# First cross-attention loop: the key projection moved two batches ahead, between the transposes and the products with the values

## The reference, cut to what matters

```python
Q = (query @ w_q.T).reshape(b, sq, NUM_HEADS, D_K).transpose(0, 2, 1, 3)
K = (key @ w_k.T).reshape(b, sk, NUM_HEADS, D_K).transpose(0, 2, 1, 3)
V = (value @ w_v.T).reshape(b, sk, NUM_HEADS, D_K).transpose(0, 2, 1, 3)
scores = jnp.einsum('bhqd,bhkd->bhqk', Q, K) / scale
scores = scores + _alibi_bias(sq, sk, scores.dtype)[None]
attn = jax.nn.softmax(scores, axis=-1)
ctx = jnp.einsum('bhqk,bhkd->bqhd', attn, V).reshape(b, sq, D_MODEL)
return ctx @ w_o.T + b_o
```

## Time and profile before

| | us |
|---|---|
| Median of three runs | 1930.89 |
| Their lowest and highest | 1924.9, 1931.84 |
| The profiled execution | 1929.83 |
| Span of its trace | 1928.2 |
| PE busy over the span | 1672.4 (87%) |
| DVE, ACT, POOL busy | 1059.2, 755.5, 746.0 |

### The profile page before, as it was taken

How to read it: one execution, slowest core, us unless ns; L and a number is a source line. 1 busy time by engine, 2 the same in 40 slices (tenths; PEclk the granted TensorE clock), 3 DMA queues, 4 the chain that set the end, 5 groups by cost and what they waited for, 6 DMA issues and landing times.

```text
span 1928.2 us, 24024 instructions
## 1 busy us (share of the span) xinstructions
PE 1672.4 (87%) x8816; PEld 806.3 (42%) x8816; DVE 1059.2 (55%) x1548; ACT 755.5 (39%) x1191; POOL 746.0 (39%) x452
## 2 busy tenths in 40 slices
PE   7888886886999999999997769999803979899998
PEld 4666663541222232222224525444401557644443
DVE  2444444465998998998993333222368464422121
ACT  1333332275776776776771222111414240122121
POOL 0433331238998998998993010000000023000000
PEclk8999997788999999999999668999855879699999
DMA  2111101003000100100102400111071100100110
GB/s 68 33 33 33 33 27 53 0 14 104 8 19 7 28 16 8 30 13 8 31 5 67 176 0 1 49 33 33 15 168 39 33 0 1 45 9 35 44 44 22
DMA packets 37895, 66.64 MB, mean 35 GB/s; under 512 B 13764, under 2 KB 24408, under 8 KB 36260
## 3 DMA queue, kind: packets, MB, share of 16 engines
q1 hardware_dynamic: 34612, 64.47, 11.3%
q10 hardware_dynamic: 3200, 1.07, 0.2%
HBM read 56.33 MB, written 9.20 MB: 34 GB/s over the span
## 4 chain that ended last, share of the span: by engine, by line
PE 51%; POOL 22%; DVE 12%; issue 11%; DMA 2%; ACT 2%; SPq 1%; DVEq 0%; ACTq 0%; POOLq 0%
POOL arena L1247 20%; PE ps L1467 6%; PE ps L2203 6%; PE ps L2214 6%; PE ps L201 3%; PE ps L1480 3%; PE ps L342 3%; PE ps L347 3%; PE ps L224 3%; PE ps L360 2%; DVE arena L477 2%; PE ps L1978 2%; PE ps L1994 2%; DVE arena L488 1%; PE ps L217 1%
## 5 line engine op out<-in xcount | busy, mean ns | idle before, releaser
L1247 POOL TENSOR_TENSOR arena<-arena 128x768 f32<-128x768 f32 x248 | 532.4, 2187 | 23.2 <-DVE arena L1164 23.2
L867 PE MATMUL ps<-arena 32*128 32x512 f32 x1520 | 316.7, 653 | 0.9 <-ACT arena L1052 0.9
L1167 DVE TENSOR_TENSOR arena<-arena,ps 128x1024 f32<-128x1024 f32 x248 | 302.1, 1218 | 10.2 <-POOL arena L1247 5.5
L2160 POOL TENSOR_TENSOR arena<-arena 128x1024 f32<-128x1024 f32 x16 | 30.0, 1896 | 433.3 <-DVE arena L2093 418.6
L1045 ACT ACTIVATE arena<-arena 128x1024 f32<-128x1024 f32 x124 | 131.1, 1057 | 136.3 <-DVE arena L1147 136.3
L1147 DVE TENSOR_TENSOR arena<-arena,ps 128x1024 f32<-128x1024 f32 x124 | 151.4, 1221 | 22.0 <-PE ps L878 9.5
L915 PE MATMUL ps<-arena 128*32 128x512 f32 (+15 forms) x1024 | 136.9, 607 | 10.4 <-DVE arena L1167 9.9
L1052 ACT ACTIVATE arena<-ps 128x1024 f32<-128x1024 f32 x124 | 127.0, 1024 | 24.8 <-PE ps L867 9.7
L1054 ACT ACTIVATE arena<-arena 128x1024 f32<-128x1024 f32 x124 | 131.1, 1057 | 3.9
L1467 PE MATMUL ps<-arena 128*128 128x512 f32 x288 | 131.9, 602 | 0.5 <-ACT arena L1532 0.5
L867 PEld LDWEIGHTS ps<-arena 32*128 32x128 f32 x1520 | 103.3, 186 | 65.3 <-issue 58.6
(11 more groups left out here) (306 smaller groups left out, 2400.6 us busy)
## 6 DMA issues: line engine op xcount, KB each, us to landing
arena<-ctxT SPq DMA_DIRECT2D x32, 257.0 KB, 3.0
arena<-ctxT SPq DMA_DIRECT2D x8, 1028.0 KB, 15.7
arena<-L_ffn_w SPq DMA_DIRECT2D x16, 512.0 KB, 4.3
arena<-ctx_rows SPq DMA_DIRECT2D x8, 960.0 KB
arena<-L_ffn_eW SPq DMA_DIRECT2D x8, 512.0 KB, 3.7
m_rows<-arena SPq DMA_DIRECT2D x12, 256.0 KB, 2.8
arena<-m_rows SPq DMA_DIRECT2D x32, 64.0 KB
m_yd<-arena SPq DMA_DIRECT2D x64, 32.0 KB, 2.3
```

The costliest lines, as they stand in the source:

```text
L867: mm = nc.tensor.matmul(ps[:, bank + jj, :], weights[r], m_row[r, n // CH % 2, n % CH, :], start=start, stop=True)
L1167: nc.vector.tensor_tensor(m_h[:, u, n % 2], m_xa[:, u, n % 2], ps[:, bank:bank + 2, :], ALU.add).then_inc(S["m_use"], 1)
L1247: nc.gpsimd.tensor_tensor(x, x, m_h[:, u, (n - 1) % 2].rearrange("p j d -> p (j d)")[:, own], ALU.mult).then_inc(S["m_kept"], 1)
```

## The change

- PE's list for a batch is now: scores of b + 1, transposes of b, keys of b + 2, value products of b, values of b + 2. Before the loop the keys and values of batches 0 and 1 are both projected.
- The keys of the 256 first context rows go to one bank (6) and the values to bank 4, which the transposes use too. So the transposes of b now also wait until the values of b + 1 have been copied out.
- The key of the last context row is projected ahead of the loop for all batches, with the last value row (eight more small matrix instructions in the trace). It is put into column 256 of `kT` by a new POOL copy of 128x2 elements for each batch, behind the query blocks, and the wait for the queries counts three events instead of two. POOL begins its first query block only when these projections have been copied out.
- DVE's list becomes: maxima of b + 1, copy of the transposed half of b, reciprocal of b + 1, output of b, copy of the values of b + 2. ACT's: copy of the transposed half, exponentials, copy of the keys.

```diff
+            for n, w in enumerate((x0["wv"], x0["wk"])):
+                for m in range(DC):
+                    o = (DC * n + m) * B
+                    for k in range(DC):
+                        mm = nc.tensor.matmul(ps[:, 0, o:o + B], w[:, k, m * P:(m + 1) * P],
+                                              x0["cl"][:, k, :], start=(k == 0), stop=(k == 1))
...
-            with pe.Fori(0, B // 2 - 1) as i:
-                b = 2 * i
-                proj(b + 1, 1, i)
-                scores(b + 1, 1)
-                tail(b, 0)
-                proj(b + 2, 0, i + 1)
-                scores(b + 2, 0)
-                tail(b + 1, 1)
-            proj(B - 1, 1, B // 2 - 1)
+            keys(1, 1, 0)
+            values(1, 1)
+            with pe.Fori(0, B // 2 - 1) as i:
+                for j in range(2):
+                    b = 2 * i + j
+                    scores(b + 1, 1 - j)
+                    turn(b, j)
+                    keys(b + 2, j, i + 1)
+                    weigh(b, j)
+                    values(b + 2, j)
...
+                nc.gpsimd.tensor_copy(x0["kT"][j][:, :, SK - 1:SK], x0["kl"][:, :, bass.ds(b, 1)]).then_inc(S["x_qblk"], 1)
```

More of the change, by code:

```diff
@@ L57 @@
 SHARED = ([(0, f"slot_ctx{j}", f"x_ctx{j}", 16 * (B // 2)) for j in range(2)]
-         + [(0, "tile_qblk", "x_qblk", DC * B), (0, "tile_norm", "x_norm", B), (0, "tile_rec", "x_rec", B)]
+         + [(0, "tile_qblk", "x_qblk", (DC + 1) * B), (0, "tile_norm", "x_norm", B), (0, "tile_rec", "x_rec", B)]
          + [(0, "once_1", "x_vl", 1), (0, "once_2", "x_vlast", 1)]
@@ L280, in build @@
             slope=bview(22 * K + 16, 4, P), pos=bview(22 * K + 16 + 256, SK + 1),
-            cl=view(37 * K, DC, B), vl=view(37 * K + 64, DC, B),
+            cl=view(37 * K, DC, B), vl=view(37 * K + 64, DC, B), kl=view(37 * K + 128, DC, B), vkl=view(37 * K + 64, 2 * DC * B),
             slope32=view(36 * K, 4, P), pos32=view(36 * K + 512, SK),
@@ L325, in x_pe, with keys, values @@
             pe.wait_ge(*S.at("xq_ev_d", 4))
[L327 to L330, removed]
-            mm.then_inc(S["x_vl"], 1)
-            def proj(b, j, i):
+            for n, w in enumerate((x0["wv"], x0["wk"])):
[4 more added lines that the diff above has]
+                                              x0["cl"][:, k, :], start=(k == 0), stop=(k == 1))
+            mm.then_inc(S["x_vl"], 1)
+            def keys(b, j, i):
+                pe.wait_ge(*S.at(f"x_ctx{j}", 16 * (i + 1)))
+                if not isinstance(b, int) or b >= 1:
+                    pe.wait_ge(*S.at("x_kev", b))
+                for m in range(DC):
+                    for k in range(DC):
+                        mm = nc.tensor.matmul(ps[:, 6, m * (SK - 1):(m + 1) * (SK - 1)], x0["wk"][:, k, m * P:(m + 1) * P],
+                                              x0["ctx"][j][:, k, 0:SK - 1], start=(k == 0), stop=(k == 1))
+                mm.then_inc(S["x_k"], 1)
+            def values(b, j):
                 if not isinstance(b, int) or b >= 1:
                     pe.wait_ge(*S.at("x_vev", b))
[L337 to L344, removed]
                 for t in range(2):
                     for k in range(DC):
-                        mm = nc.tensor.matmul(ps[:, 6, t * D:(t + 1) * D], cx[:, k, t * P:(t + 1) * P],
+                        mm = nc.tensor.matmul(ps[:, 4, t * D:(t + 1) * D], x0["ctx"][j][:, k, t * P:(t + 1) * P],
                                               x0["wv"][:, k, :], start=(k == 0), stop=(k == 1))
@@ L353, in scores @@
                 pe.wait_ge(*S.at("x_kev", b + 1))
-                pe.wait_ge(*S.at("x_qblk", 2 * b + 2))
+                pe.wait_ge(*S.at("x_qblk", 3 * b + 3))
                 if not isinstance(b, int) or b >= 1:
@@ L366, in scores, with turn @@
                 mm.then_inc(S["x_s"], 1)
-            def tail(b, j):
+            def turn(b, j):
                 pe.wait_ge(*S.at("x_norm", b + 1))
+                pe.wait_ge(*S.at("x_vev", min(b + 2, B) if isinstance(b, int) else b + 2))
                 for t in range(2):
@@ L376, in tail, with weigh @@
                     mm.then_inc(S["x_pt"], 1)
+            def weigh(b, j):
                 pe.wait_ge(*S.at("x_or", b + 1))
@@ L386, in tail @@
                 mm.then_inc(S["x_o"], 1)
-            proj(0, 0, 0)
+            keys(0, 0, 0)
+            values(0, 0)
             pe.wait_ge(*S.at("x_alibi", 4))
             scores(0, 0)
+            keys(1, 1, 0)
+            values(1, 1)
             with pe.Fori(0, B // 2 - 1) as i:
-                b = 2 * i
-                proj(b + 1, 1, i)
-                scores(b + 1, 1)
-                tail(b, 0)
-                proj(b + 2, 0, i + 1)
-                scores(b + 2, 0)
-                tail(b + 1, 1)
-            proj(B - 1, 1, B // 2 - 1)
+                for j in range(2):
[5 more added lines that the diff above has]
+                    values(b + 2, j)
             scores(B - 1, 1)
-            tail(B - 2, 0)
-            tail(B - 1, 1)
+            turn(B - 2, 0)
+            weigh(B - 2, 0)
+            turn(B - 1, 1)
+            weigh(B - 1, 1)
             pe.wait_ge(*S.at("x_or", B + 1))
@@ L423, in keys @@
                 act.wait_ge(*S.at("x_k", b + 1))
-                nc.scalar.copy(x0["kT"][j], ps[:, 4:6, 0:SK]).then_inc(S["x_kev"], 1)
+                nc.scalar.copy(x0["kT"][j][:, :, 0:SK - 1],
+                               ps[:, 6, :].rearrange("p (m s) -> p m s", m=DC)).then_inc(S["x_kev"], 1)
             def exps(b, j):
@@ L439, in x_act @@
             exps(0, 0)
+            keys(1, 1)
             with act.Fori(0, B // 2 - 1) as i:
[L441 to L448, removed]
+                for j in range(2):
+                    b = 2 * i + j
+                    turned(b)
+                    exps(b + 1, 1 - j)
+                    keys(b + 2, j)
             turned(B - 2)
@@ L465, in x_dve @@
             ch.link(nc.vector.tensor_reduce(x0["par"], hmask.rearrange("p (a i) -> p i a", i=2), AX.X, ALU.add))
-            nc.vector.tensor_copy(x0["vl"].rearrange("p c b -> p (c b)"), ps[:, 0, 0:DC * B]).then_inc(S["x_vlast"], 1)
+            nc.vector.tensor_copy(x0["vkl"], ps[:, 0, 0:2 * DC * B]).then_inc(S["x_vlast"], 1)
             for r in (slice(0, 6), slice(64, 70)):
@@ L472, in values @@
                 dve.wait_ge(*S.at("x_v", b + 1))
-                nc.vector.tensor_copy(x0["v"][j].rearrange("p a b -> p (a b)"), ps[:, 6, :]).then_inc(S["x_vev"], 1)
+                nc.vector.tensor_copy(x0["v"][j].rearrange("p a b -> p (a b)"), ps[:, 4, :]).then_inc(S["x_vev"], 1)
             def maxima(b, j):
@@ L484, in sums, with turned, outs @@
                 nc.vector.reciprocal(x0["st"][j][:, 2, :], x0["st"][j][:, 1, :]).then_inc(S["x_rec"], 1)
-            def outs(b):
+            def turned(b):
                 dve.wait_ge(*S.at("x_pt", 2 * b + 2))
                 nc.vector.tensor_copy(x0["pT"][:, 1, :], ps[:, 5, :]).then_inc(S["x_pt1ev"], 1)
+            def outs(b):
                 dve.wait_ge(*S.at("x_o", b + 1))
@@ L501, in x_dve @@
             sums(0, 0)
+            values(1, 1)
             with dve.Fori(0, B // 2 - 1) as i:
[L503 to L512, removed]
+                for j in range(2):
+                    b = 2 * i + j
+                    maxima(b + 1, 1 - j)
+                    turned(b)
+                    sums(b + 1, 1 - j)
+                    outs(b)
+                    values(b + 2, j)
             maxima(B - 1, 1)
+            turned(B - 2)
+            sums(B - 1, 1)
             outs(B - 2)
-            sums(B - 1, 1)
             dve.wait_ge(*S.at("x_norm", B))
@@ L520, in x_dve @@
                                         x0["own"].unsqueeze(1).broadcast_to([P, B, L]), ALU.mult).then_inc(S["x_spread"], 1)
+            turned(B - 1)
             outs(B - 1)
@@ L558, in normed @@
                                         ALU.mult).then_inc(S["x_norm"], 1)
+            pool.wait_ge(*S.at("x_vlast", 1))
             qblk(0, 0)
```

## The result

| | before | after |
|---|---|---|
| Median of the runs | 1931.19 us (4 runs) | 1896.52 us (4 runs) |
| Lowest to highest | 1924.9 to 1931.84 | 1893.49 to 1897.95 |
| Profiled execution, its span | 1929.83, 1928.2 | 1896.26, 1894.6 |
| Scores of batch 1 to scores of batch 31 | 244.10 | 208.75 |

The ratio after to before is 0.9826, with an interval of 0.9802 to 0.9849: the changed kernel is faster by 1.7%. The gain is 34.7 us by the medians where 29 had been forecast.

What follows compares the result with a forecast made beforehand. PE was taken to bound the loop; its terms summed to 7.16 us per batch against 8.137, so 1929.83 - 29.3 + 0.9 = 1901.4 us, stated as 1902 for the median, range 1896 to 1911.

Steps and rivals of the forecast that it cites:

- PE bounds the loop and loses time at L383 and at the branch: In the loop: PE is busy 14.55 of 16.28 us per two batches and loses time between its instructions.
- Both waits go: Before the value products: PE's waits for ACT's copy (0.40 us) and DVE's copy (0.30 us) should vanish.
- The branch goes under: At the loop's end: the branch's 0.38 us per pair of batches is hidden behind the values, taken as 0.
- Scores 1.70, transposes 0.96, keys 1.84, values 1.94: PE's forecast us per batch for these four pieces of the loop in the new order.
- rival B: In PE's loop: the new seams between pieces are dear, giving 7.40 us per batch and 1909 us; chance 0.12.
- Value products 0.72: In PE's loop: each half of the value products costs 0.36 us once unhindered, 0.72 us per batch.
- 1898 to 1910 of the bounds: Whole kernel: time in us by the bounds alone, with a batch between 7.04 and 7.40 us.
- Ahead of the loop + 0.9: Before the loop: eight more small instructions on PE's path add 0.9 us, upper bound 1.08.
- Nothing else is late: In the loop: softmax, copies and transfer finish before they are wanted, the softmax with 1.2 us to spare.
- POOL's copy 0: In the loop: the new 128x2 copy runs in POOL's idle 4.75 us per batch, 0 on the path.
- D: In the loop: PE's clock falls to 1.2 GHz, making the kernel slower, 1942 to 1959 us; chance 0.03.
- Later stages only shift: Behind the loop: later stages are taken as shifted only, without changing their lengths.

Runs made afterwards that it cites:

- experiment 1: Changed kernel with the keys of b + 2 put back behind the value products; 1925.9 us, ratio to before 0.9983.
- experiments 2 and 3: PE's loop written as 5 turns of 6 batches: in the kernel before, 1925.2 us; in the changed kernel, 1894.1 us.
- experiment 8: Changed kernel with keys and value products cut in halves and interleaved; 1906.3 us, ratio to before 0.9865.
- experiments 5 and 6: Changed kernel with DVE's output ahead of its reciprocal again, 1898.3 us; or with one more POOL instruction between reciprocal and scaling, 1897.6 and 1903.1 us.
- experiment 7: Changed kernel with three more POOL instructions between reciprocal and scaling of each batch; 1913.7 us.
- experiment 4: Changed kernel with keys and values of b + 2 exchanged, values between transposes and value products, keys last; 1924.9 us, ratio to before 0.9979.

## Why the prediction was right, and where its sizes were off

- *PE bounds the loop and loses time at L383 and at the branch.* Right: with these gone PE is busy 140.00 of 140 us.
- *Both waits go.* Right, and experiment 1 shows that the place of the keys does it. Of the 0.98 us between 7.94 and 6.96 the idle time is 0.70. The rest is overlap: transposes 1.10 to 0.93, value products 0.79 to 0.58, keys 1.84 to 1.82, less 0.11 that the values gained (1.82 to 1.93).
- *The branch goes under.* Right: 0.38 before, nothing after (experiments 2 and 3). Why it shows behind the small products is not settled: either these fill the queue and hold the branch back, or the 0.36 us of work left after their last wait is simply too short to cover a branch. No run here tells the two apart. The Trainium skill's figure of 64 queue entries ("TensorE: Matmul & The Clock Gate", section "Architectural detail: the array is 16× 32×32, not 1× 128×128"), quoted in the prediction, fits the first: the 64 instructions of the held-up products would fill it.
- *Scores 1.70, transposes 0.96, keys 1.84, values 1.94.* Measured 1.70, 0.93, 1.82, 1.93. The upper bounds that I kept for transposes and keys (rival B) were not needed.
- *Value products 0.72.* The term that was mis-sized: 0.58. I doubled the 0.36 of one half, which is the price of 16 small products that stand alone; experiment 8 shows 0.36 each apart and 0.58 together. 0.14 x 30 = 4.2 of the 6.0 us by which the loop beat the sum (7.16 to 6.96). As I gave this term no lower bound, the loop fell below the lowest sum of 7.04, and the time below the 1898 to 1910 of the bounds. That the stated range from 1896 on still held is partly luck: two of the changed kernel's eight runs (1893.49 and 1891.43) lie under it.
- *Ahead of the loop + 0.9.* The small products did cost 0.90 more (1.81 instead of 0.91). In the profiled execution the scores of batch 1 start 3.19 later: another 0.60 because all began later (37.17 against 36.57), and 1.66 for the first keys at the lower clock. Both come and go between executions of the changed kernel's beginning, so the term of 0.9 stands. The two traces with the old beginning have no slow keys, too few to say that the change does not make them likelier.
- *Nothing else is late.* Right: the softmax ends 1.0 us before it is wanted (I had 1.2, of a period of 7.16), and experiments 5 and 6 use 0.57 of that without loss. The sum for the copied keys, 3.42 + 0.59, is 4.0 and not 4.1; in the trace their copy ends 4.0 behind the scores, and the next scores begin at 5.26. The price beyond the slack was wrong by a factor of two (experiment 7).
- *POOL's copy 0.* Right: 0.19 us each, while POOL waits. *Clock* (D): 1.00 throughout the loop.
- *Later stages only shift.* Right as far as the traces show. From the first products behind the loop (L410, now L418) to the end of the span it is 1622.8 us before and 1621.4 after. The spans agree: they differ by 33.6 us, the loop brings 35.35 and the beginning gives back 3.19, so 1.4 us more arose behind the loop, where the code is the same; the changed kernel's own runs lie 4.5 us apart, and I leave that open.

## What to carry to other kernels

When an engine waits for another to copy out its last result, put its next independent piece there, but check both ends of the move: experiment 4 filled the same gap and opened another of 0.87 us, because the moved piece's own reader came next. Take the price of a group from a row in which it stands as it will stand in the new order: here small products next to their like were cheaper than two groups apart (0.58 against 0.72 us), and a group that is split paid for each change of kind. Where a piece of the next round stands between a result and its use, as the scores do here, a chain that is too long is paid only half: 0.34 of 0.67 us in experiment 7.

## What was not expected of the hardware

- 16 small products (128x32 weights, 64 columns) took 0.36 us between full-size ones, 32 together 0.58; one more round trip from full-size products to small ones and back cost 0.34 us.
- The loop's branch on PE cost 0.38 to 0.44 us behind 32 held-up small products and 0 behind 1.93 us of full-size ones.
- The clock under the first key projection was at the lower level in two of nine executions with the same code ahead of it, worth 1.66 us.
